# A two-layer transformer with mixture gates: the opening and the start of each layer's attention laid out anew

## The reference, cut to what matters

```python
x = L0_attn_x
xn = _layernorm(x, axis=-1)
s = _L0_attn_ref(xn, ...)             # 16 heads of 8 features, rotated q and k, causal over 1024 rows
g = _silu(_L0_ffn_ref(xn, ...))       # soft mixture: 8 experts x 64 slots, hidden width 512
x = x + s * g
xn = _layernorm(x, axis=-1)
s = _L1_attn_ref(xn, ...)             # the same attention with other weights
g = _silu(_L1_ffn_ref(xn, ...))       # 16 experts, routed, then a layer norm
x = x + s * g
...
# in the soft mixture
xn = rmsnorm(x, norm_gamma)           # x / |x| * sqrt(128) * gamma
sn = rmsnorm(slot_embeds, slot_norm_gamma)
logits = jnp.einsum('bnd,esd->bnes', xn, sn)
dispatch = jax.nn.softmax(logits, axis=1)
combine = jax.nn.softmax(logits.reshape(b, n, e * s), axis=-1)
slots = jnp.einsum('bnd,bnes->besd', xn, dispatch)
h = _gelu(jnp.einsum('besd,edh->besh', slots, w1) + b1)
eo = jnp.einsum('besh,ehd->besd', h, w2) + b2
out = jnp.einsum('bmd,bnm->bnd', eo, combine)
```

## Time and profile before

| | us |
|---|---|
| median of 3 runs | 819.37 |
| lowest, highest | 805.48, 820.41 |
| the profiled execution | 810.94 |
| its span (first to last instruction) | 809.1 |
| PE busy | 688.0 |
| DVE busy | 512.5 |
| ACT busy | 450.7 |
| POOL busy | 286.5 |
| mean granted clock of PE | 0.878 |

### The profile page before, as it was taken

The page is one execution under the profiler, slowest core; times in us unless marked ns, Lnnn a source line. Parts: engine busy times, 40 slices in busy tenths (PEclk is TensorE's granted clock), DMA queues, the critical chain, the costliest instruction groups (busy, mean ns, idle before and its releaser), DMA issues.

```text
span 809.1 us, 14402 instructions
## 1 busy us (share of the span) xinstructions
PE 688.0 (85%) x5166; PEld 328.1 (41%) x5166; DVE 512.5 (63%) x844; ACT 450.7 (56%) x896; POOL 286.5 (35%) x488
## 2 busy tenths in 40 slices
PE   3337868999979999899989999999999997999944
PEld 1125612355555336443332364334434333256613
DVE  7872398876544572577646547698899897653301
ACT  1214303655636676866656765676767774645841
POOL 3548512233100111267421114672122122015883
PEclk9558955999998999698788997899999997799965
DMA  5200563020370123003341124055132212000000
GB/s 160 68 10 1 155 169 116 28 60 27 103 188 7 35 51 78 10 1 92 122 112 43 47 61 152 2 139 147 46 86 60 56 32 61 1 1 2 1 26 27
DMA packets 33476, 52.24 MB, mean 65 GB/s; under 512 B 5888, under 2 KB 24064, under 8 KB 30848
## 3 DMA queue, kind: packets, MB, share of 16 engines
q1 hardware_dynamic: 32112, 50.87, 23.3%
q10 hardware_dynamic: 1296, 0.46, 0.2%
HBM read 37.42 MB, written 13.63 MB: 63 GB/s over the span
## 4 chain that ended last, share of the span: by engine, by line
PE 60%; DVE 16%; POOL 10%; issue 6%; ACT 5%; DMA 2%; POOLq 0%; SPq 0%; ACTq 0%; DVEq 0%
PE ps L1184 55%; DVE maxes L1170 6%; ACT probs L922 3%; DVE rope L1034 2%; POOL gate L462 2%; PE ps L1390 1%; DMA F<-in_w 1%; PE ps L1277 1%; POOL gate L799 1%; POOL gate L810 1%; ACT F L882 1%; POOL gate L811 1%; PE ps L1238 1%; DVE kop L1039 1%; PE ps L1293 1%
## 5 line engine op out<-in xcount | busy, mean ns | idle before, releaser
L1170 DVE TENSOR_REDUCE maxes<-ps 128x2 f32<-128x1024 f32 (+2 forms) x288 | 339.9, 1221 | 116.2 <-PE ps L1184 114.1
L922 ACT ACTIVATE probs<-ps 128x512 f32<-128x512 f32 x576 | 306.0, 603 | 119.4 <-PE ps L1184 118.6
L1184 PE MATMUL ps<-qop,kop 74*128 74x512 bf16 (+3 forms) x768 | 193.0, 351 | 13.8 <-ACT probs L922 7.0
L775 POOL TENSOR_SCALAR_AFFINE_SELECT probs<-probs 128x512 f32<-128x512 f32 (+1 forms) x160 | 83.5, 544 | 264.3 <-ACT probs L922 264.0
L1184 PE MATMUL ps<-probs,vgrp 128*32 128x512 f32 (+3 forms) x1536 | 160.2, 528 | 12.8 <-POOL probs L775 11.3
L1184 PE MATMUL ps<-kmx,qmx 32*128 32x128 bf16 (+2 forms) x1280 | 109.7, 282 | 27.5 <-DVE maxes L1170 14.8
L1184 PEld LDWEIGHTS ps<-qop,kop 74*128 74x128 bf16 x768 | 62.9, 103 | 119.5 <-ACT probs L922 60.3
L1184 PE MATMUL ps<-F 128*128 128x128 f32 (+3 forms) x768 | 93.5, 285 | 6.1 <-DMA F<-in_w 3.3
L1184 PEld LDWEIGHTS ps<-F 128*128 128x128 f32 (+2 forms) x768 | 85.6, 185 | 24.8 <-issue 16.3
L1184 PEld LDWEIGHTS ps<-kmx,qmx 32*128 32x128 bf16 x1280 | 39.1, 94 | 135.2 <-issue 77.0
L1184 PEld LDWEIGHTS ps<-probs,vgrp 128*32 128x32 f32 x1536 | 39.2, 113 | 73.9 <-issue 53.1
(11 more groups left out here) (154 smaller groups left out, 685.9 us busy)
## 6 DMA issues: line engine op xcount, KB each, us to landing
qop<-q_thirds SPq DMA_DIRECT2D x48, 192.0 KB
kop<-k_thirds SPq DMA_DIRECT2D x48, 192.0 KB
qmx<-q_thirds SPq DMA_DIRECT2D x16, 256.0 KB
kmx<-k_thirds SPq DMA_DIRECT2D x16, 256.0 KB
F<-in_w SPq DMA_DIRECT2D x16, 256.0 KB, 5.0
q_thirds<-third SPq DMA_DIRECT2D x8, 384.0 KB, 3.0
k_thirds<-third SPq DMA_DIRECT2D x8, 384.0 KB, 2.8
q_thirds<-third SPq DMA_DIRECT2D x8, 256.0 KB, 2.2
```

The source lines that it names most:

```text
L775: last = pool.affine_select(where, where, [[0, number], [1, P]], ALU.is_ge, 0.0, base=0, channel_multiplier=-1)
L922: act.activation(probs[:, u % RING, :], bank(at), ACT.Exp, scale=SCALE).then_inc(s_cells_read, 1)
L1170: dve.tensor_reduce(dst, src, AX.X, ALU.max).then_inc(s_units_read[pair // 2], 1)
L1184: return pe.matmul(out_, lhsT, rhs, start=first, stop=last)
```

## The change

What it does, part by part:

1. **Opening.** `stat` of chunks 0 and 1 is followed by one refinement for both together on DVE (128x2x8 instead of 128x2x4), that of chunks 2 and 3 is one on POOL. `xr` goes from POOL to ACT (four activations with a scale for each row); gamma is not multiplied in rows any more but is a scale for each partition in the ACT copies behind the transposes (`xrT`, `embT`, `slot`). The ones of kop are written by POOL before anything else, together with zeros in rows 64 to 127 of qop.
2. **Double rotated rows.** `rope` holds two chunks and the sine products have a tile of their own, `sine`. The rotation of chunk c waits for the sum of chunk c - 1 and for `low` of chunk c - 2. In layer 0 the sum is DVE's.
3. **First shift by halves.** In groups 0 and 8 (`SPLIT`), `top`, the split (`halve`) and `shift` are done for the first 512 query rows after 6 of the 18 `max` units, and for the rest after all 18. `PATTERN` is reordered so that the first three entries hold all of the first half. `exp` of the first half waits for the first part alone.
4. **Whole slots.** `slot` makes 128 columns in one product instead of 64 twice.
5. **pv without a copy.** `vals` itself is the stationary operand, 9 columns wide; `vg` is gone, and DVE clears the PSUM bank once at the start.
6. **exp over 128 rows.** kop and qop are taken whole instead of 74 rows.
7. **The end.** `heads` is done in halves of four row tiles, and the last two adds are DVE's.
8. **Order.** The model's steps are finer (`lt` and its exponential, `diag` and its sum, `heads` and its reciprocal apart), a ring's bank counts as held until it is read, and the model of PE's speed is another; ORDER comes out otherwise in many places.

```diff
-PATTERN = [[(i, 0, 512)] for i in (4, 5, 6, 7)] + [
-    [(2, 0, 256), (3, 0, 256)], [(6, 512, 256), (7, 512, 256)],
-    [(1, 0, 128), (3, 256, 128), (5, 512, 128), (7, 768, 128)],
-    [(i, P * i, 128) for i in range(4)], [(i, P * i, 128) for i in range(4, 8)]]
-NM = 2 * len(PATTERN)
+PATTERN = [[(2, 0, 256), (3, 0, 256)], [(1, 0, 128), (3, 256, 128), (5, 512, 128), (7, 768, 128)],
+           [(i, P * i, 128) for i in range(4)]] + [[(i, 0, 512)] for i in (4, 5, 6, 7)] + [
+    [(6, 512, 256), (7, 512, 256)], [(i, P * i, 128) for i in range(4, 8)]]
+NM, DIAGONAL = 2 * len(PATTERN), (2, 8)
+SPLIT = (0, 8)
+UNITS_DONE = {0: 6, 1: NM, 2: NM}
...
+            pool.memset(kop[64:P].rearrange("p r h t -> p (r h t)").bitcast(F32), ONES).then_inc(s_ones, 1)
+            pool.wait_ge(s_ones, 1)
+            pool.memset(qop[64:P].rearrange("p r h t -> p (r h t)").bitcast(F32), 0.0).then_inc(s_ones, 1)
...
+                elif what == ("root", 0, 1):
+                    for c in range(2, 4):
+                        pool.wait_ge(s_stat, NTH["stat", 0, c])
+                    refine(pool, own, *(root[:, :, n, 8:16] for n in range(3))).then_inc(s_root, 1)
...
-                    pool.wait_ge(s_f0, 48)
-                    pool.wait_ge(s_norm, NTH["norm", 0, c, 3])
-                    for t in range(4 * c, 4 * c + 4):
-                        last = pool.tensor_scalar(xr[:, t, :], xn[:, t, :], root[:, 1, 1, t:t + 1], None, ALU.mult)
-                    own.link(last)
-                    pool.tensor_tensor(xr[:, four, :], xr[:, four, :], gam0[:, 0:1, :].to_broadcast([P, 4, E]),
-                                       ALU.mult).then_inc(s_xr, 1)
...
+                elif kind == "xr":
+                    c, = arg
+                    act.wait_ge(s_norm, NTH["norm", 0, c, 3])
+                    for t in range(4 * c, 4 * c + 4):
+                        last = act.activation(xr[:, t, :], xn[:, t, :], ACT.Copy, scale=root[:, 1, 1, t:t + 1])
+                    last.then_inc(s_xr, 1)
...
                     if L or c:
-                        dve.wait_ge(s_low, NTH[("low", L, c - 1, n) if c else ("low", 0, 3, n)])
+                        dve.wait_ge(s_summed[L if c else 0], NTH[("sum", L, c - 1, n) if c else ("sum", 0, 3, n)])
+                    if L or c >= 2:
+                        dve.wait_ge(s_low, NTH[("low", L, c - 2, n) if c >= 2 else ("low", 0, c + 2, n)])
...
+                elif kind == "sum" and not arg[0]:
+                    L, c, n = arg
+                    made = UNIT["qk", L, c, n]
+                    dve.wait_ge(s_units_read[made % 2], made // 2 + 1)
+                    dve.tensor_tensor(rope[:, c % 2, n, :], rope[:, c % 2, n, :], sine[:, n, :], ALU.add).then_inc(s_summed[0], 1)
                 elif kind == "embstat":
-                    for r in range(2):
-                        dve.memset(kop[64:KM, r], 1.0).then_inc(s_ones, 1)
                     dve.wait_ge(s_emb_in, 16)
...
-                        last = mm(bank(at)[:, 0:SL0], xr[:, u // NB0 * TB + i, :], disp[:, u % 2, i, SL0 * half:SL0 * half + SL0],
-                                  i == 0, i == TB - 1)
+                        last = mm(quarter(at, 0), xr[:, u // NB0 * TB + i, :], disp[:, u % 2, i, :], i == 0, i == TB - 1)
...
                     if u == 0:
                         pe.wait_ge(s_xload[r], 96 * (n // 2 + 1))
-                        pe.wait_ge(s_shift_in[r], 32 * (n // 2 + 1))
+                    if u in FIRST_UNIT and (n in SPLIT or u == 0):
+                        for half in (FIRST_UNIT.index(u),) if n in SPLIT else (0, 1):
+                            pe.wait_ge(s_shift_in[half][r], 16 * (n // 2 + 1))
                     for j, h, q, w, c in UNITS[u]:
-                        last = mm(bank(at)[:, c:c + w], kop[0:KM, r, h, P * j:P * j + P], qop[0:KM, r, h, q:q + w])
+                        last = mm(bank(at)[:, c:c + w], kop[:, r, h, P * j:P * j + P], qop[:, r, h, q:q + w])
...
-                            last = mm(ps[VP * h:VP * h + VP, 7, q % BANK:q % BANK + w], vgrp[:, n % 2, j, h, :],
+                            last = mm(ps[VP * h:VP * h + VC, 7, q % BANK:q % BANK + w], vals[:, n // GB % 2, j, n % GB * HG + h, :],
                                       probs[:, u % RING, c:c + w], j == 0, step == HALF_END[half] and j == keys[-1])
```

399 lines of the change are left out of this document (246 added, 153 removed), and 1 row of the table COST.

## The result

| | before | after |
|---|---|---|
| median, us | 813.63 (4 runs, 805.48 to 820.41) | **783.95** (4 runs, 782.46 to 787.61) |
| ratio | | 0.970, 95% interval 0.964 to 0.977 |
| profiled execution, its span | 810.94, 809.1 | 782.46, 780.7 |
| first load of the attention | 87.84 | 50.30 |
| first max unit | 99.17 | 59.66 |

The rows from the profiled execution down to `eo` are of the two profiled executions, in us from the start of the span. 783.95 over 813.63 is 0.964; the ratio of 0.970 compares fast executions alone, and the kernel before has a slower state (819.37 and 820.41 here, against 805.48 and 807.89).

What follows compares the result with a forecast made beforehand. Waiting between engines was taken to bound the kernel up to 132.5, PE behind it. Span 809.1 - 46 (opening, kept at `eo`) - 1 - 6 (end) = 756, 758 with 1.8 outside, median 762; range 730 to 796.

Steps and rivals of the forecast that it cites:

- The opening to the max units: Start of the kernel: first load at 49 (before 87.84), first max unit at 55, by the rows' gap 60.
- the sums on DVE: Rotation sums in the opening, moved from POOL: taken as 0.75, bounds 0.6 to 1.26; contention could cost 4 us.
- The first exp: End of the opening: first exp from 132.50 to 79.5, -53; bounds 70.5 and 87.
- First exp to `eo`: Stretch to the experts' second products of layer 0: PE busy 102, idle 2, so 104 us, ending at 183.5.
- Slots: Slots between first exp and `eo`: from 4 x 3.76 to 5 x 2.05, -4.8 us on PE.
- Behind `eo`: Rest of the run: -1 from fewer units left to do and -6 at its end.
- The end: Last masks: PE's 10.56 us wait filled by later attention products; -6 in all, between -14 and +3.
- rival D: Planner's order loses elsewhere: PE's 36 us idle between 229.6 and 720 doubles, giving 798; chance 0.05.
- rival B's good side: PE's clock, wait gone and full-height exps: up to 60 us low clock vanish, giving 732; chance 0.30 with bad side.
- 9 columns: pv products, width 32 to 9: group stays at 160.2, no gain counted; shorter weight loads might give 752.
- E: Slower: 9-column products keep PE at half clock through all of pv, giving 917; chance 0.03.
- 128 rows: exp products over 128 rows instead of 74: group stays at 193.0, no gain counted.

Runs made afterwards that it cites:

- a_best: Changed kernel, planner's list with PE always fast, SP's queue thinned ahead of the shift, end's masks, adds, silu moved, qop's zeros by DVE: 750.52 us, ratio 0.920.
- a_shift_first: Changed kernel with the first half of the first shift issued ahead of the stores of chunk 2 on SP's queue: 781.19 us, ratio 0.956.
- a_lean: Changed kernel with the first half-shift issued ahead of group 1's six loads, three weight loads and the stores of chunk 2: 779.83 us, ratio 0.959.
- a_nosplit: Changed kernel without the shift by halves, the planner making a new list: 774.77 us, ratio 0.951.
- a_noclock: Changed kernel with a new list from the planner, which takes PE for fast throughout; same work: 759.22 us, ratio 0.933.
- a_tail: Changed kernel with the end reordered: a last-group mask ahead of POOL's adds and last layer norm steps, last silu behind the last exponential: 775.63 us, ratio 0.949.
- a_spread7_again: Second run of the changed kernel with `lg` 6 moved next to its reader and group 7's 17 max units spread between group 6's exps: 772.85 us, ratio 0.953.
- a_74: Changed kernel with exp over 74 rows again instead of 128: 805.14 us, ratio 0.984.
- b_exp128: Kernel before, in its own order, with exp over 128 rows instead of 74: 787.50 us, ratio 0.967.
- b_pv9: Kernel before, in its own order, with pv products of 9 columns instead of 32, DVE clearing the PSUM bank once: 815.44 us, ratio 0.998.
- a_closed: Changed kernel with `lg` 6 and group 7's max units moved, the end reordered and SP's queue thinned ahead of the first shift: 762.38 us, ratio 0.939.
- a_single: Changed kernel with each chunk's rotation waiting for `low` of the chunk ahead, as with one buffer; new list: 753.45 us, ratio 0.931.

## Why the prediction was off

In short: four steps failed. The shift's transfer was held by the transfers ahead of it and not by its turn in the queue, which put the first exp 6.7 us late. The path from there to `eo` was taken as PE's work with 2 us of idle time, and took 9.5 longer. The wait at the end was taken as filled, and wasn't (8.3). And a loss by the order elsewhere had a chance of 0.05 and no term in the sum (12.1). A gain that the sum hadn't, the clock that the full rows keep up (19), nearly covered the last two.

**The opening to the max units: right.** First load 49 forecast, 50.30 measured; first max unit 55 by the sum, 60 by the gap of the rows, 59.66 measured. One step in it was wrong by 3.5 us: both chunks were to be normalised by 14, and it was 17.5 (15.39 + 2.13). POOL's memset of qop ran from 6.43 to 9.94, and DVE's operation of 128x4, begun at 6.84, ended at 9.96: 3.12 instead of 0.17. In `a_best`, where DVE writes these zeros itself at the start, the same operation takes 0.17, and both chunks are normalised by 15.74 although DVE begins 1.9 later:

```profile
8.00 0.17 DVE L1126 TENSOR_SCALAR root<-root 128x4 f32<-128x4 f32 x1
...
13.60 2.14 DVE L537 TENSOR_SCALAR xn<-x,mv,root 128x128 f32<-128x128 f32 x8
```

I had used that behaviour for POOL's addition and had priced the memsets at nothing as POOL was free. What covers a step on its own engine does not cover what it does to another. Of the sums on DVE, bound 0.6 to 1.26 and taken as 0.75, two took 1.29: 0.65 each. The contention that the Trainium skill names for two SBUF inputs (page "GPSIMD Engine Reference", section "1. Specifications") did not cost them anything here: POOL stood idle between 29.10 and 30.87, while they ran.

**The first exp: 6.7 late.** Forecast 79.5, measured 86.22, inside its bounds. The first load was 1.3 late; from it to the shift's issue it took 32.5 us (50.30 to 82.81) instead of 28.9, 3.6 more; and the landing took 3.4 instead of 1.5, 1.9 more. The step that failed is what these terms stand for: I let the shift wait for its turn in SP's queue, and counted the loads as issues, not as bytes under way. Issued 6.4 us earlier, the shift landed no earlier (9.7 us, `a_shift_first`), and with fewer transfers ahead of it it took at most 4.5 (`a_lean`).

**First exp to `eo`: 104 forecast, 113.5 measured.** PE was busy 106.0 (102 in the sum) and idle 7.5 (2). The granted clock was 0.92 in this stretch, 0.96 in the one before; that is some 10 us more at 1.2 GHz (length times 2 times the missing share), an estimate that would cover the 4 us. The wrong step is deeper than the 9.5: I made the gain at `eo` hang on the first exp. `a_nosplit` and `a_lean` move the first exp by 19 us and `eo` by 6. What stays nearly fixed, in lists with the same work between, is the distance from the first max unit: 136 to 142 us, and 146 in `a_noclock`, where PE idled 13.61 for the shift. Before it was 130.4, with four `lt` and four slots done ahead of it, against three and one here. Counted from the first max unit, 39.5 earlier, with the 9.6 more, the 29.9 at `eo` comes out. The shift by halves, which gives the exps an earlier start by 12 us, gave 3 at `eo`, and its list was 9 us slower in the end.

**Slots: right.** They take 2.02 to 2.05 whole at full clock; one, at 70.29, fell into the low clock and took 3.78.

**Behind `eo`: -7 forecast, +1.5 measured.** Three parts. *The end* I took as filled. It was not: PE waited 2.90 and 9.50, since I read that more products stood there and did not read that the masks they need stood behind the adds and the layer norm on POOL. In the earlier trace rows the releaser was POOL; where it stands in POOL's list was the thing to look up. 8.3 us by `a_tail`. *The order elsewhere*, rival D, had a chance of 0.05 and happened: 12.1 by `a_spread7_again`. I had PE's idle time of the earlier trace rows as the only sign; the list of the changed kernel had `lg` 6 116 places ahead of its reader for all to see. *The clock*, rival B's good side, was also true: 19 us by `a_74`, 23 by `b_exp128`, but it only paid for the other two, and it came from the rows of the exp products and not from the filled wait. So D and B happened together, where I had treated them as alternatives. The account isn't closed: with the rows' gain left out, 20.7 us were lost where 7 were to be gained, and of these 27.7 the two repairs explain 20.4.

**9 columns: right** at none, E is out: the pv group isn't longer, 153.1 against 160.2, and `b_pv9` at 0.998 [0.992, 1.004] leaves neither loss nor a gain of over 1%. **128 rows: right** at none for a product at full clock, wrong for the kernel.

**The sum.** Forecast span 756, measured 780.7: 16.2 of the 24.7 ahead of `eo` (6.7 at the first exp, 9.5 in the stretch behind it), 8.5 behind it. `a_closed` at 762.38 is the forecast's number. That is luck in part: it has 19 us from the rows that the sum hadn't, and at `eo` (194.36) it is still 11 late. And that 783.95 lies in the range at all is owed to those 19 us too: without them `a_74` stands at 805.14, outside it.

**What stays open.** The distance from the first max unit to `eo` is 140 here and 127.5 in `a_single` (64.92 to 192.46, PE busy 110.61 at a clock of 0.92). Its list has less work on the way, 72 max units instead of 81 and 70 exps instead of 74, and PE is busy 10.3 us less; what else shortens it isn't settled by a run of its own. `a_nosplit`'s 9 us lie behind `eo` (569.2 against 581.0) and go with another list; which place of it gives them I did not look for, and the hole before group 7 is there too (62 us apart). Nor does any run separate rows from their contents: the added rows always held zeros and ones.

## What to carry to other kernels

A list that is written ahead of time is itself a part of the cost: nearly the same work took 784, 775, 759 or 753 us by the list (in the second without the shift by halves, in the last with one more wait), more than most edits of the work were worth. After any change to a planner, look in its list for a step that holds a scarce buffer while its reader stands far behind, and for what stands ahead of the masks, norms and transfers on which PE waits. Take the gain of a faster opening at the point where the shared work begins (here the first max unit), and count an earlier first result only for the idle time of the bounding engine that it fills. And try to fill empty rows of the array where that costs no columns, then read the clock before and after.

## What the runs showed of the hardware

- Exp products over 128 rows instead of 74, with zeros and ones in the added rows, take the same 226 ns at full clock (the median from one start to the next), but in the kernel before the granted clock behind `eo` goes from 0.90 to 0.95 and the time to 0.967 [0.961, 0.974] of it. Taking them back in the changed kernel lowers the clock there from 0.94 to 0.88 (`a_74`). I had mainly the idle waits in mind as the cause of the low stretches.
- pv products on 9 columns instead of 32 did not lower it (`b_pv9`, 0.90 as before, 0.998 [0.992, 1.004]).
- A transfer of 8 KB issued behind twelve of 192 KB was used 9.7 us after its issue (`a_shift_first`), 16.8 us in `a_noclock` (78.34 to 95.17), at most 4.5 with six of them ahead of it (`a_lean`). Such a backlog also stretched the issuing of four stores from 3.26 us (`a_lean`) to 11.91.
- A DVE operation of 128x4 that takes 0.17 took 3.12 beside a POOL memset and ended with it (9.96 and 9.94), and 0.17 again where POOL had no such memset (`a_best`); the memset has no input at all, and the operation one.
